# Row sums of two units on ScalarE, written orders for TensorE, ScalarE and VectorE, and values and sums in one group

## The reference, cut to what matters

```python
scores = jnp.einsum('bnqd,bnkd->bnqk', q, k) * scale
scores = jnp.where(causal, -jnp.inf, scores)
attn = jax.nn.softmax(scores, axis=-1)
out = jnp.einsum('bnqk,bnkd->bnqd', attn, v)
...
gate = jnp.einsum('bsd,hd->bsh', x, w_gate)
up = jnp.einsum('bsd,hd->bsh', x, w_up)
return jnp.einsum('bsh,dh->bsd', _silu(gate) * up, w_down)
```

## Time and profile before

| | us |
|---|---|
| median of 3 runs | 2075.26 (2074.24 to 2076.37) |
| the profiled execution, its span | 2071.9 |
| TensorE matmuls busy | 2014.1 (97%) |
| VectorE, ScalarE, GpSimd busy | 1175.5, 750.5, 998.2 |
| attention part of the second iteration | from 555.6 to 772.3 |

### The profile page before, as it was taken

The page is one execution under the profiler, slowest core; times in us unless marked ns, Lnnn a source line. Parts: engine busy times, 40 slices in busy tenths (PEclk is TensorE's granted clock), DMA queues, the critical chain, the costliest instruction groups (busy, mean ns, idle before and its releaser), DMA issues.

```text
span 2071.9 us, 34740 instructions
## 1 busy us (share of the span) xinstructions
PE 2014.1 (97%) x10560; PEld 1440.7 (70%) x10560; DVE 1175.5 (57%) x2428; ACT 750.5 (36%) x1349; POOL 998.2 (48%) x775
## 2 busy tenths in 40 slices
PE   7999999999999999999989999999999999999998
PEld 6555488888755558888765555888887555588887
DVE  5767454445676745454457674545456767444554
ACT  1357432221145652222114665222221466432221
POOL 4224259763312436975331243697533223279743
PEclk9999999999999999999999999999999999999999
DMA  5333101111333311111243331011113333111112
GB/s 155 90 83 73 32 32 61 52 61 41 84 73 83 73 38 35 62 52 52 72 134 73 83 73 42 32 62 52 52 42 83 73 83 73 42 41 61 52 52 82
DMA packets 59177, 134.11 MB, mean 65 GB/s; under 512 B 10720, under 2 KB 11744, under 8 KB 58976
## 3 DMA queue, kind: packets, MB, share of 16 engines
q1 hardware_dynamic: 58976, 131.66, 22.6%
HBM read 76.57 MB, written 4.19 MB: 39 GB/s over the span
## 4 chain that ended last, share of the span: by engine, by line
PE 88%; issue 4%; DVE 4%; ACT 2%; DMA 1%; POOL 1%; DVEq 0%; SPq 0%; POOLq 0%; ACTq 0%
PE bank L1469 11%; PE bank L1333 11%; PE bank L1335 11%; PE bank L1334 11%; PE ring L1333 10%; PE ring L1334 9%; PE ring L1335 9%; PE ring L1411 8%; PE bank L1442 7%; PE ring L1324 1%; DVE xn L1062 1%; ACT prob L820 1%; DMA x<-x_in 1%; DMA area<-nm_lo 0%; DVE stats L994 0%
## 5 line engine op out<-in xcount | busy, mean ns | idle before, releaser
L1062 DVE CUSTOM_DVE_ANT_0 xn<-ring,mask_row 128x128 bf16<-128x128 f32 (+1 forms) x448 | 308.7, 710 | 90.4 <-PE ring L1411 85.7
L699 POOL TENSOR_SCALAR_AFFINE_SELECT prob<-prob 128x512 f32<-128x512 f32 x128 | 81.3, 635 | 524.4 <-ACT prob L820 404.0
L820 ACT ACTIVATE prob<-bank 128x512 f32<-128x512 f32 (+1 forms) x512 | 265.4, 569 | 187.8 <-PE bank L1442 185.8
L622 POOL TENSOR_SCALAR area<-w_stage 128x1024 fp32r<-128x1024 f32 x129 | 139.5, 1081 | 371.5 <-PE bank L1335 203.0
L624 POOL TENSOR_TENSOR area<-w_stage,area 128x1024 fp32r<-128x1024 f32 x129 | 308.9, 2395 | 10.8
L1135 DVE TENSOR_TENSOR x<-x,bank 128x512 f32<-128x512 f32 x256 | 170.9, 685 | 233.3 <-PE bank L1335 233.3
L1333 PE MATMUL ring<-xt_hi,area 128*128 128x512 f32 x672 | 266.6, 397 | 3.7 <-DVE area L1168 1.3
L1334 PE MATMUL ring<-xt_lo,area 128*128 128x512 f32 x672 | 263.0, 391 | 0.0
L1335 PE MATMUL ring<-xt_hi,area 128*128 128x512 f32 x672 | 263.0, 391 | 0.0
L1411 PE MATMUL ring<-area 96*128 96x512 f32 (+3 forms) x768 | 239.5, 374 | 13.8 <-DVE row_max L1062 11.7
L1411 PEld LDWEIGHTS ring<-area 96*128 96x128 f32 x768 | 129.4, 189 | 156.7 <-DVE row_max L1062 104.1
(11 more groups left out here) (166 smaller groups left out, 3532.9 us busy)
## 6 DMA issues: line engine op xcount, KB each, us to landing
w_stage<-ffn_w SPq DMA_DIRECT2D x96, 512.0 KB, 3.3
area<-kq_parts SPq DMA_DIRECT2D x336, 128.0 KB, 2.3
w_stage<-attn_w SPq DMA_DIRECT2D x35, 512.0 KB, 3.4
area<-attn SPq DMA_DIRECT2D x48, 128.0 KB, 2.3
x<-x_in SPq DMA_DIRECT2D x20, 256.0 KB, 3.9
out<-x SPq DMA_DIRECT2D x16, 256.0 KB, 2.2
bias_rows<-row_bias SPq DMA_DIRECT2D x10, 256.0 KB, 4.0
area<-nm_hi SPq DMA_DIRECT2D x32, 8.0 KB, 1.8
```

The source lines that it names most:

```text
L622: pool.tensor_scalar(hi, src, 1.0, 0.0, ALU.mult, ALU.add).then_inc(w_hi_done, 1)
L699: pool.affine_select(out=tile, in_=tile, compare_op=ALU.is_ge, fill=0.0, base=0, pattern=[[0, GH], [1, P]], channel_multiplier=-1).then_in ...
L820: act.activation(prob[:, step % 2, h, off:], scores_at(u, j, h), ACT.Exp, scale=SCALE).then_inc(prob_ready, 1)
L1062: dve.tensor_tensor_reduce(out=sum_out[:, RING[name] % 2, 0:keys], in0=src[:, 0:keys], in1=mask_row[:, TOKENS - keys:], scale=1.0, scalar= ...
```

## The change

`SUMMED` becomes (3, 5): unit 3 is done as unit 5 is. `weigh` is called for values and sums of a key tile together in every unit (`MERGED` holds them all). `UNIT_START`, `STEP_PARTS`, `POINTS` and their relatives go; in their place each engine has one string for each unit. In `ORDER` (TensorE) s is the next `scores_t`, v the next group of `weigh` and f the next of `fill_of` (projections, s1, mt, output projections, ln2). In `ACT_ORDER` e is the next exponential, r the next row sum, x the next evacuation or `qk_to_hi`. In `DVE_ORDER` m is the next of the ring, q a `qk_to_lo`, r a part of a reciprocal, h a `shift`. What each engine does is the same but for unit 3; the two copies of ln2 on ScalarE come after the last exponential of unit 7. `PROB_BUFS` is 2, as before.

```diff
-SUMMED = (5,)
+SUMMED = (3, 5)
+PROB_BUFS = 2
-POINTS = {0: (0, 1, 2, 3, 4, 6, 8, 10, 11), ...
-BETWEEN = {0: (2, 1, 2, 1), 1: (2, 1, 2, 1), 3: (2, 1, 2, 1), 5: (2, 1, 2, 1)}
-STEP_PARTS = (((0,), ("values",), (1,), ("sums",)), ((0,), (1,), ("values", "sums"), ()),
-              (("head 0", "head 1"), ("values",), ("head 2",), ("head 3",)))
-UNIT_START = (
...
+def fill_of(u):
+    if u == UNITS - 1:
+        return (("op", 0, 0, 3), ("op", 1, 0, 3), ("op", 0, 3, 4), ("op", 1, 3, 4), ("op", 2, 0, 4), ("op", 3, 0, 4),
+                ("ln2", 0), ("ln2", 1))
+    other = list(beside(u))
...
+    parts = [("project", u + 2, w, k, k + 2) for w in range(2) for k in (0, 2)]
...
+def weighed(u, j):
+    return (("values", "sums"),) if narrow(u, j) or u in SUMMED or (u, j) in MERGED else (("values",), ("sums",))
+MERGED = [(u, j) for u in range(8) for j in range(8)]
+ORDER = (
+    "ffffffffffsfssfsfssfsvfsssfssfvfssfssfvfffff",
+    "sfsvfssfsfsfsfsfvsfsfsfsfvfsfsfsfsvfsfssfsfvsfssfsfvfsssfsvssssff",
+    "svvsfsffsfffssvfssfsssfsvsfsssffvvfff",
+    "ssffssffsfsfsfsvfsfsvsfsfssffsfsfsvfsfsvsfsfssfssvfsssfvfssssvf",
+    "sfssvfffffssssfsfvfsssfsfsfsvssfvvfffvffff",
...
+)
+ACT_ORDER = (
+    "xeexeeeeeeeeee",
+    "eexeeeexxeeeeeeeeeereeeerreeerrereereer",
+    "eerrxxeerxeerreererreeex",
+    "eeexeeexeeeeeeeeeeeeereeeerereerere",
+    "errrxxerexeeeeerrreerrrreex",
...
+)
+DVE_ORDER = (
+    "mmmqmmmmmqmmmmmmm",
+    "mmmmrmmmrqmmqmmmrmmmrmmmmmmmrmmmmrrmmrmrr",
+    "mmmmmmrrhrmrr",
+    "mrmmmrmmqmmrmmrqmmmmmmrrmmmmmmrmmmrrm",
...
+)
@@ scalar, iteration
+                    for what in ACT_ORDER[u]:
+                        if what == "e":
+                            exps(*next(weights))
+                        elif what == "r":
+                            u_sum, t = next(rows)
+                            row_sums(u_sum, t)
+                            if t == GH * CT - 1:
+                                row_logs(u_sum)
...
+                xt_to_hi(it, ("ln2", 0))
+                xt_to_hi(it, ("ln2", 1))
                 evacuate(UNITS - 1)
@@ tensor, iteration
+                    for what in ORDER[u]:
+                        if what == "s":
+                            scores_t(*next(score))
+                        elif what == "f":
+                            name, *which = next(fill)
+                            run[name](*which)
+                        else:
+                            v_unit, j, kinds = next(group)
+                            for kind in kinds:
+                                weigh(v_unit, j, kind)
```

More of the change, by code:

```diff
@@ L218 @@
[L218 to L225, removed]
+PROB_BUFS = 2
[5 more added lines that the diff above has]
+    other = list(beside(u))
+    if u == UNITS - 2:
+        return tuple(other)
+    parts = [("project", u + 2, w, k, k + 2) for w in range(2) for k in (0, 2)]
+    if u + 2 not in SIDE_UNITS:
+        return (*parts, *(one for one in other if one != ("mt", u + 1)))
+    lead = other[:2], other[2:3], other[3:5], other[5:6]
+    if u % 2:
+        lead = (("mt", u), *lead[0]), *lead[1:]
+    elif other[-1] == ("mt", u + 1):
+        other = other[:-1]
+    return (*(x for p, some in zip(parts, lead) for x in (p, *some)), *other[6:])
@@ new lines, in iteration @@
+                for n, (what, *which) in enumerate(beside(-1)):
+                    take[what](*which)
+                    if n in TAKE_AFTER:
+                        take_v(CT + 2 + TAKE_AFTER.index(n))
+                drain = iter([one for u in range(UNITS - 1)
+                              for one in (*([("lo", u + 2, w) for w in range(2)]
+                                            if u < UNITS - 2 and u + 2 not in SIDE_UNITS else ()), *beside(u))])
+                low = iter([(u, w) for u in SIDE_UNITS for w in range(2)])
@@ new lines, in iteration @@
+                inverse = iter([(u, n) for u in range(UNITS - 2) if u not in SUMMED for n in range(RECIPS)])
+                shifted = iter(SUMMED)
+                take["lo"] = qk_to_lo
+                for u in range(UNITS - 1):
+                    for what in DVE_ORDER[u]:
+                        if what == "m":
+                            name, *which = next(drain)
+                            take[name](*which)
+                        elif what == "q":
+                            qk_to_lo(*next(low))
+                        elif what == "h":
+                            shift(next(shifted))
+                        else:
+                            v_unit, n = next(inverse)
+                            recip_part(v_unit, n)
+                            if n == RECIPS - 1:
+                                normalise_attn(v_unit)
```

192 lines of the change are left out of this document (33 added, 159 removed).

## The result

| | us | ratio to before, 95% |
|---|---|---|
| before, 4 runs | 2075.01 | |
| changed kernel, 4 runs | 2046.38 (2044.64 to 2047.36) | 0.9855 (0.9841 to 0.9869) |
| forecast | 2035 (2008 to 2056) | |
| changed kernel, its profiled span | 2042.9 | |

A forecast was written before the change was run, and what follows sets the result against it. TensorE's matmuls, busy 97% of the span, were taken as the bound. Per iteration 6.77 + 3.2 = 10.0 us off, waits summing to 0; four iterations -40.0 from 2071.9 gives 2031.9, plus 3.4 for the median: 2035 us (2008 to 2056).

The forecast's parts named there:

- Sums of unit 3, -27.1 us: TensorE in unit 3: its eight groups of sums go, saving 6.77 us an iteration, 27.1 us in four.
- Joining, -12.9 us: TensorE: 17 entries and exits saved an iteration, 14 by joining values and sums, at 0.19 us each; 12.9 us in four.
- a rival, with 0.05: Joining saves nothing, as the drain is overlapped or scores wait longer for exponentials: 2048 us, chance 0.05.
- Row sums hidden on ScalarE: Sixteen row sums an iteration, 15.6 us in all, fit ScalarE's free time between exponentials and cost nothing.
- Shift of unit 3, +1 us an iteration: TensorE waits before unit 3's transpose, as its maxima now come through ScalarE: 0.2 to 2 us, taken as 1.
- Unit 5, -2 us: Spreading VectorE's load removes 2 of unit 5's 3.1 us of TensorE idle an iteration, bounds 0 and 3.
- The 0.92 us before its transpose: TensorE's idle time between unit 5's last row sum and its transpose, 0.92 us, expected to stay.
- Scores behind the stacked rows of units 3 and 7, +0.5 us: After mt of units 3 and 7, 3.4 us of work precede the scores against 3.65: 0.25 us each, 0.5 an iteration.
- SyncE and GpSimd have the same lists; the weight splits stay where they were: SyncE's and GpSimd's instruction lists were taken as unchanged; no cost was put on them in the sum.
- where 9 were foreseen: Sign of being right: units 0 to 5 together some 9 us shorter an iteration, units 6 and 7 some 1.3 us.
- The row of waits before the groups' weight loads: TensorE's weight loads idle before 32-column matmuls, 73.5 us, 272 times, read as 68 group entries an iteration.
- A count of 184 entries and about 50 us: Sign of being right: entries before groups fall from 272 to about 184, their idle time from 73.5 to about 50 us.

The follow-up runs named there:

- later splits: Changed kernel, with GpSimd's weight splits ahead of units 2, 3 and 4 waiting for VectorE's multiplication of units 0, 1 and 2: 2033.25 us.
- the sums of unit 3 back: Changed kernel with later splits, unit 3's sums back on TensorE joined to its values, its row sums off ScalarE: 2064.30 us.
- both edits in the old orders: Kernel before, with unit 3 without sums on TensorE and full key tiles joined, old orders on all three engines: 2100.59 us.
- two masked buffers: Changed kernel with later splits, two buffers of masked scores instead of three and three buffers of exponentials instead of two: 2067.32 us.

## Why the prediction was right or wrong

- **Sums of unit 3, -27.1 us: right in the new orders.** Unit 3 is 5.4 us shorter without seven of its eight groups, where 6.8 were put on all of them apart and some 5.6 would be the price joined. In the old orders the same edit is worth nothing. The claim "work on the bounding engine, with no cover to lose" holds only when the order is made anew: at 97% busy the engine still had places where it would have waited.
- **Joining, -12.9 us: the price of one pair somewhat too low (0.24 to 0.27 for 0.19), but the step counted no cost for what joining does to the scores around it.** In the two tiles of unit 1 above the waits for exponentials take all of it, 4.03 us against 3.96. The forecast had that only as a rival, with 0.05.
- **Row sums hidden on ScalarE: right**, within 1 us.
- **Shift of unit 3, +1 us an iteration: right in size, not in place.** TensorE does not wait at the transpose, as the forecast had it; transposed scores of unit 2 wait, as their exponentials stand on ScalarE behind the last row sums and the logarithms, 0.85 us of idle in the second iteration:

```profile
633.30 0.44 PE L1415 MATMUL bank<-area 98*128 98x128 f32 x2 [0.85 <-ACT prob L804]
```

- **Unit 5, -2 us: right**, its idle fell by 2.6. The 0.92 us before its transpose, which were to stay, are among what went.
- **Scores behind the stacked rows of units 3 and 7, +0.5 us: too high**, 0.2 us in the iteration shown.
- **"SyncE and GpSimd have the same lists; the weight splits stay where they were": the step that failed.** It was true of the lists and wrong to count it as no cost. VectorE's list had moved beside GpSimd's, and the multiplication, which reads SBUF twice, does not run beside GpSimd's subtraction: 1.94, 2.90 and 2.42 us where 0.69 were counted. Moving the splits brought 13 us, more than the 11.4 us that were missing; with it the kernel stands at 2033, by the forecast's 2035. That is partly luck: units 0 to 5 are 6.9 us shorter there (157.0 to 150.1) where 9 were foreseen, and units 6 and 7 2.7 us (47.3 to 44.6) where 1.3 were. Where the second comes from no run shows.
- **The row of waits before the groups' weight loads was misread.** "A count of 184 entries and about 50 us" was said to show the step right; the changed kernel has

```profile
PEld bank L1442 <- issue: 70.8, 270, 0.4
```

  though its list has 44 entries an iteration for 66. Before it was 66 and not the 68 that 272 / 4 gave. Pauses of the weight loads inside joined groups are in the row too: the run with 19 more pairs joined in the old orders has fewer entries than before, 47 an iteration in its trace, and 337 in the row.

```profile
PEld bank L1469 <- issue: 93.8, 337, 0.4
```

  So neither the count nor its 0.27 us was one of entries. The distances of starts carried the sum, and they held.

## What to carry to other kernels

When an order moves work on one engine, check what then runs at the same time on the engine that shares memory access with it, even if that one's list isn't touched: look at the instructions with two SBUF inputs on VectorE, and at all on GpSimd that read SBUF. Taking work from the bounding engine pays only where its order has something else ready; laid into the old order, edits worth 27 and 14 us by their distances gave 0 and a loss of 31. Price a joined block by the period of the loop it stands in, and count the buffers that the other engines can work on while it runs.

## What the runs showed of the hardware

A two-input VectorE multiplication that begins beside a two-input subtraction on GpSimd ends only 0.5 us after it: 2.90, 2.42 and 1.94 us for 0.69 alone, and 2.51 us for a quarter of the columns, while the subtraction keeps its 2.4 us. In the other order GpSimd loses: a one-input conversion that begins while a multiplication runs takes 1.05 us for 0.62. Maxima with one operand in PSUM keep their length beside the same subtraction.

Some kernels with more waits also had more time at the lower clock level of 1.2 GHz: the mean granted clock, as a share of 2.4 GHz, was 0.999 for the changed kernel and the one with later splits, 0.995 with the sums of unit 3 back and with both edits in the old orders, 0.992 with two masked buffers. With the sums of unit 3 back, the stretch of unit 4, where TensorE is idle for 2.8 of 28.4 us, has 0.94; all stretches shown of the changed kernel have 1.00. An estimate from these shares: 0.4% of 2064 us is up to 8 us of clock in the kernel with the sums back, and 0.7% up to 14 us in the one with two masked buffers. That much of their time may be clock and not waits.
